# A transformer block with shared and routed experts on one core: expert weights loaded whole, the stage ahead of the tiles put in another order, and the weight and destination of each routed row formed on VectorE instead of GpSimd

## What is computed

```python
h = _layernorm(x) * (1 + ca) + sa
x = x + ga * attention(h)
h = _layernorm(x) * (1 + cb) + sb
out = silu(h @ sg.T) * (h @ su.T) @ sd.T                  # shared expert
probs = softmax(h @ wr.T + rb); scores, idx = top_k(probs, 2); scores /= scores.sum()
for e in range(7):
    out = out + w[..., e] * (silu(h @ rg[e].T) * (h @ ru[e].T) @ rd[e].T)
x = x + gb * out
```

## Time and profile before

| | |
|---|---|
| median of 3 runs | 798.48 us (797.54 to 799.52) |
| the profiled execution's own time | 797.6 us |
| its span in the trace | 795.9 us |
| busy: PE, DVE, ACT, POOL | 686.8, 573.4, 545.9, 342.0 us |
| attention / middle / tiles and the end | to 490 / 490 to 595 / 595 to 796 us |

### The profile page before, as it was taken

The page is one execution under the profiler, slowest core; times in us unless marked ns, Lnnn a source line. Parts: engine busy times, 40 slices in busy tenths (PEclk is TensorE's granted clock), DMA queues, the critical chain, the costliest instruction groups (busy, mean ns, idle before and its releaser), DMA issues.

```text
span 795.9 us, 18082 instructions
## 1 busy us (share of the span) xinstructions
PE 686.8 (86%) x5304; PEld 395.3 (50%) x5304; DVE 573.4 (72%) x2042; ACT 545.9 (69%) x1013; POOL 342.0 (43%) x551
## 2 busy tenths in 40 slices
PE   2986899999999999999999986678869989999970
PEld 1553123333333333333333434567659889999960
DVE  5797889999999999999999834574773323333543
ACT  2785259889989888989888788544325556666640
POOL 1367613232322322232322123235657887666652
PEclk9999569999999999999999999699999999999995
DMA  9246021111111111111110079202233322223425
GB/s 260 83 156 219 1 74 47 39 30 29 47 47 48 47 28 30 41 46 47 48 37 14 1 136 178 68 23 81 63 92 78 82 76 81 66 68 104 131 87 158
DMA packets 64760, 59.46 MB, mean 75 GB/s; under 512 B 10798, under 2 KB 52398, under 8 KB 64668
## 3 DMA queue, kind: packets, MB, share of 16 engines
q1 hardware_dynamic: 58924, 46.85, 23.3%
q0 software_dynamic: 4480, 9.64, 3.4%
q10 hardware_dynamic: 1264, 1.84, 0.7%
HBM read 33.57 MB, written 24.33 MB: 73 GB/s over the span
## 4 chain that ended last, share of the span: by engine, by line
PE 59%; DVE 18%; ACT 9%; issue 7%; DMA 3%; POOL 1%; SPq 1%; ACTq 1%; DVEq 0%; POOLq 0%
PE ps L1658 13%; PE ps L1602 10%; PE ps L1843 9%; PE ps L1681 7%; PE ps L1854 6%; DVE junk L1238 5%; ACT probs L973 5%; PE ps L1864 3%; PE ps L1758 2%; PE ps L1636 2%; DVE junk L1210 2%; PE ps L1750 2%; DMA routed_results_scratch<-y_s,s_dest 1%; PE ps L1831 1%; DVE rot L1193 1%
## 5 line engine op out<-in xcount | busy, mean ns | idle before, releaser
L973 ACT ACTIVATE probs<-ps 128x1024 f32<-128x1024 f32 (+1 forms) x320 | 285.5, 941 | 34.5 <-PE ps L1681 32.1
L1210 DVE CUSTOM_DVE_ANT_0 junk<-ps,tri 128x512 f32<-128x512 f32 (+3 forms) x512 | 218.5, 487 | 13.9 <-PE ps L1602 11.6
L1602 PE MATMUL ps<-ka,qa 61*128 61x256 bf16 (+3 forms) x788 | 186.7, 325 | 10.0 <-DVE rowmax L1210 3.0
L775 POOL TENSOR_SCALAR_AFFINE_SELECT probs<-probs 128x512 f32<-128x512 f32 x128 | 79.7, 634 | 191.8 <-ACT probs L973 191.8
L1658 PE MATMUL ps<-probs,v 128*32 128x512 f32 (+3 forms) x1536 | 157.7, 498 | 1.3 <-POOL probs L775 1.1
L1681 PE MATMUL ps<-qa,ka 64*128 64x512 bf16 (+3 forms) x768 | 144.6, 331 | 7.7 <-ACT probs L973 5.6
L1602 PEld LDWEIGHTS ps<-ka,qa 61*128 61x128 bf16 x788 | 53.0, 95 | 159.8 <-DVE rowmax L1210 80.4
L844 POOL DMA_INDIRECT routed_results_scratch<-y_s,s_dest x76 | 76.2, 1003 | 41.0 <-issue 35.0
L782 POOL DMA_INDIRECT slot_rows_scratch<-rows,slot x64 | 64.1, 1001 | 56.6 <-DVE slot L1393 30.1
L1243 DVE TENSOR_REDUCE leftmax<-ps 128x1 f32<-128x512 f32 x120 | 78.4, 686 | 8.5 <-PE ps L1602 8.5
L1532 DVE TENSOR_TENSOR hid_s<-sg,ps 128x352 f32<-128x352 f32 x76 | 39.6, 521 | 46.2 <-ACT sg L1087 46.0
(11 more groups left out here) (195 smaller groups left out, 1168.4 us busy)
## 6 DMA issues: line engine op xcount, KB each, us to landing
slot_rows_scratch<-cst SPq DMA_DIRECT2D x1, 5396.0 KB, 36.1
srow<-slot_rows_scratch SPq DMA_DIRECT2D x76, 71.0 KB
k_parts_scratch<-qk_parts SPq DMA_DIRECT2D x12, 320.0 KB, 2.7
ka<-k_parts_scratch SPq DMA_DIRECT2D x32, 120.0 KB
q_parts_scratch<-qk_parts SPq DMA_DIRECT2D x12, 256.0 KB, 2.6
qa<-q_parts_scratch SPq DMA_DIRECT2D x32, 96.0 KB
ka<-k_parts_scratch SPq DMA_DIRECT2D x32, 80.0 KB
xs<-in_x SPq DMA_DIRECT2D x4, 512.0 KB, 9.4
```

Of the source, the lines that this page charges most:

```text
L775: nc.gpsimd.affine_select(out=p, in_=p, compare_op=ALU.is_ge, fill=0.0, base=0, pattern=[[0, HQ], [1, T]], channel_multiplier=-1).then_inc ...
L973: nc.scalar.activation(probs[(n * NS + s) % 4][:, 2 * h:2 * h + 2, 0:UNTIL[s] - FROM[s]], ps[:, 2 * h:2 * h + 2, FROM[s]:UNTIL[s]], ACT.Ex ...
L1210: last = V.tensor_tensor_reduce(out=junk[:, bank - 5, at:at + w], in0=ps[:, bank, at:at + w], in1=tri[:, CH - w:CH], scale=1.0, scalar=LOW ...
L1602: last = MM(ps[:, bank, at:at + w], qa[m][g0:g0 + KS, c0 + q * T:c0 + (q + 1) * T], ka[m][g0:g0 + KS, d0 + k0:d0 + k0 + w], start=True, st ...
```

## The change

- Middle: the lists of calls of TensorE, VectorE and ScalarE are written in another order. `gate_up` and `silu` may now be called for single pieces, and `hidden(0, 0)` comes before the routing of the first half.
- Weights: `w_whole` holds all seven experts (it lies where `w_lo` lies, which is formed in place). SyncE loads all of it in one go, behind the end of attention and ahead of `wd`; nothing is loaded late in attention, and no load waits for a buffer.
- Tiles: the register load, `s_weight` and `s_dest` go from GpSimd to the end of VectorE's step, one step list of VectorE beginning at -2. Destinations are now computed as floating point and written as integers, and the constants are stored so.

```diff
+        w_whole = sb("w_whole", [D, NE, 2, NI], at=before_y)
+        before_y.close()
         w_lo = sb("w_lo", [D, NE, 2, NI], F32R, at=moe)
...
-            load_expert(0)
-            load_expert(1)
-
             sp.wait_ge(s_ring_free, len(BY_DVE))
+            for e in range(NE):
+                sp.dma_start(w_whole[:, e, 0, :], sw_g_d[1 + e, :, :]).then_inc(s_wraw[e], 16)
+                sp.dma_start(w_whole[:, e, 1, :], sw_u_d[1 + e, :, :]).then_inc(s_wraw[e], 16)
             for c, (i0, w) in enumerate(IC):
                 sp.dma_start(wd[0:w, :, c, :], sw_d_d[1:EX, i0:i0 + w, :].rearrange("e p h -> p e h")).then_inc(s_wd, 16)
-            for e in range(2, NE):
-                load_expert(e)
...
-            pool.wait_ge(s_expert, GRP)
-
             def slot_step(i, r):
-                at = tile(i, r, -2)
-                if at:
-
-                    t, j, times = at
-                    pool.wait_ge(s_srow[j], 16 * times + 16)
-                    e = pool.value_load(expert[0:1, bass.ds(t, 1)], min_val=0, max_val=NE - 1)
-                    nc.gpsimd.tensor_copy(s_weight[:, bass.ds(t, 1)], srow[:, j, bass.ds(D + e, 1)])
-                    d = (r + 2) % SU
-                    needs(pool, s_y_out[j], 16 * (times - SU // SB + 1))
-                    nc.gpsimd.tensor_tensor(s_dest[:, d:d + 1], srow[:, j, bass.ds(D + NE + e, 1)].bitcast(I32),
-                                            cst[:, bass.ds(CST["spare"][0] + t, 1)].bitcast(I32), ALU.add).then_inc(s_meta, 1)
...
+                at = tile(i, r, -2)
+                if at:
+                    t, j, times = at
+                    dve.wait_ge(s_srow[j], 16 * times + 16)
+                    e = dve.value_load(expert[0:1, bass.ds(t, 1)], min_val=0, max_val=NE - 1)
+                    V.tensor_copy(s_weight[:, bass.ds(t, 1)], srow[:, j, bass.ds(D + e, 1)])
+                    d = (r + 2) % SU
+                    needs(dve, s_y_out[j], 16 * (times - SU // SB + 1))
+                    V.tensor_tensor(s_dest[:, d:d + 1], srow[:, j, bass.ds(D + NE + e, 1)],
+                                    cst[:, bass.ds(CST["spare"][0] + t, 1)], ALU.add).then_inc(s_meta, 1)
                 if isinstance(i, int) and first_combine <= r < first_combine + 3 * GC:
                     combine(*divmod(r - first_combine, 3))
-            slot_steps(dve, -1, ST + 1, slot_step)
+            dve.wait_ge(s_expert, GRP)
+            slot_steps(dve, -2, ST + 1, slot_step)
...
             pe.wait_ge(s_ws_lo, 1)
             pe.wait_ge(s_wds_gated, len(IC))
-            gate_up(0, (0, 1))
+            gate_up(0, (0,))
+            router(2)
             router(3)
+            pe.wait_ge(s_x2, 2)
+            gate_up(0, (1, 2))
             turn_normalised(4)
-            gate_up(0, (2,))
+            gate_up(1, (0, 1))
+            down(0)
+            turn_normalised(5)
             counts(0)
```

More of the change, by code:

```diff
@@ L293, in adaln_block @@
         ws_lo = sb("ws_lo", [D, 2, NI], F32R, at=att)
-        w_raw = sb("w_raw", [D, 2, 2, NI], at=att)
+        w_raw = sb("w_raw", [D, 2, NI], at=att)
         wds = sb("wds", [128, len(IC), D], at=att)
@@ L426, in adaln_block @@
         s_exp7 = sem("s_exp7")
-        s_wraw = [sem(f"s_wraw{m}") for m in range(2)]
+        s_wraw = [sem(f"s_wraw{e}") for e in range(NE)]
         s_whi = sem("s_whi")
@@ L1017, in first_part @@
             def first_part(e):
-                act.wait_ge(s_wraw[e % 2], 32 * (e // 2 + 1))
-                nc.scalar.activation(w_hi[:, e, :, :], w_raw[:, e % 2, :, :], ACT.Copy).then_inc(s_whi, 1)
+                act.wait_ge(s_wraw[e], 32)
+                nc.scalar.activation(w_hi[:, e, :, :], w_whole[:, e, :, :], ACT.Copy).then_inc(s_whi, 1)
             def exp7(g):
@@ L1023, in exp7, with silu @@
                 nc.scalar.activation(prob[:, GTILES[g], :], logit[:, GTILES[g], :], ACT.Exp).then_inc(s_exp7, 1)
-            def silu(n):
-                for c, (i0, w) in enumerate(IC):
+            def silu(n, pieces=range(len(IC))):
+                for c in pieces:
+                    i0, w = IC[c]
                     g = n * len(IC) + c
@@ L1276, in chunk, with attended @@
                 return slice(n * CG, (n + 1) * CG)
-            b = B - 1
-            for u in range(2):
-                n = 2 * b + u
+            def attended(u):
+                n = 2 * (B - 1) + u
                 dve.wait_ge(s_proj, u + 1)
```

187 lines of the change are left out of this document (99 added, 88 removed).

## The result

Measured were **790.2 us** (median of 7 runs, 787.3 to 795.0) against 799.1 us for the kernel before in the same comparison: ratio 0.989, 95% interval 0.988 to 0.991. The sign was right and 790.2 lies in the range, but the gain is 8.5 to 9 us where 16 were forecast. The profiled execution took 790.4 us (before 797.6), its span is 788.3 us (before 795.9), so 7.6 us have to be found in the traces, and 8.4 of the forecast gain are missing there.

A forecast was written before the change was run, and what follows sets the result against it. Bounds: waits round a TensorE, ScalarE, VectorE ring in the middle; TensorE's pace in the tiles, GpSimd between tiles 12 and 23. Middle -15.4, GpSimd -1.4, VectorE +0.8 give -16.0: 797.6 becomes 781.6, about 782 us with 0.9 added; range 771 to 793.

The forecast's parts named there:

- First `hid`, 506.5: Middle: the first `hid` starts at 506.5 instead of 514.73, with logits at 506.0 and 0.5 us of `softmax_shift`.
- VectorE's work behind it, 63.7: Middle: VectorE's work and small gaps from the first `hid` to the last `xs` come to 63.7 us.
- VectorE's waits, 9 us: Middle: VectorE waits 3 to 4 us for `down`, 4 for `silu`, 1 to 2 at hand-overs: 9 us.
- priced at 1.3: Middle, ScalarE: a fifth function table load ahead of the second `hid` costs 1.3 us, within the 9 us of waits.
- Stop of TensorE behind `down(7)`: End of the middle: TensorE stands long during VectorE's list behind `slots(1)`, at no cost because VectorE is at work.
- GpSimd, -1.4 us: Tiles: GpSimd's step falls from 2.77 to 2.57 us but starts later; 5.6 us lost instead of 7.0.
- VectorE in the tiles, +0.8 us: Tiles: VectorE's new work is hidden except 0.5 us in nine last steps adding `combine` and 0.3 at tile 0.
- Weights loaded whole, 0: Middle: loading all 14 weight transfers from about 490 costs nothing, as each lands before it is read.
- The ring keeps its waits: Middle: new lists move the stops instead of filling them; end at up to 590.7, time 788 to 794; chance 0.13.
- The first half's scatters: Rival: these scatters hold the tiles, landing at 573 to 575 against 579; at 1.4 us each, 786; chance 0.08.
- the bound of the tiles: Rival: VectorE's register load sequence exceeds 1.6 us and sets the tile pace; slower from 1.8 us; chance 0.05.
- The shared port: Tiles: VectorE's new operations hold up GpSimd's scatters by 0.2 us in 19 steps, 3.8 us more, 786; chance 0.04.

The follow-up runs named there:

- rows_later: The changed kernel with GpSimd waiting for chunk 3's `h_lo` before it scales the rows of chunks 2 and 3; 786.6 us, ratio 0.9848.
- six_third: The changed kernel with counts_later, logits4_early, rows_later, `combine` ahead of `hid_s`, five `w_lo` moved earlier and second-half row scatters thinned; 774.2 us, ratio 0.9692.
- counts_later: The changed kernel with TensorE's `counts(1)` behind `down(5)` instead of ahead of `gate_up(6, (1,))`; 786.6 us, ratio 0.9838.
- logits4_early: The changed kernel with VectorE's `logits(4)` and `hidden(2, 0)` ahead of `slots(0)`; 789.1 us, ratio 0.9877.
- exp_first: The changed kernel with `exp7(0)` ahead of `silu(0, (0,))` on ScalarE and `softmax_scale(0)` ahead of `hidden(0, 0)` on VectorE; 793.7 us, ratio 0.9935.
- tiles_alone: The kernel before with only the weight column and destinations moved from GpSimd to VectorE, middle and weights as before; 797.2 us, ratio 0.9975.
- tiles_undone: The changed kernel with the weight column and destinations formed on GpSimd again, new middle and whole weights kept; 792.5 us, ratio 0.9920.
- slots1_early: The changed kernel with VectorE's `slots(1)` directly behind `starts(1)` and `experts(1)` ahead of `hidden(7, 2)`; 788.5 us, ratio 0.9871.

## Where the prediction was right and where it was wrong

The sign was right and the gain half of what was forecast. The step that failed is VectorE's waits in the middle; the others are smaller.

- **First `hid`, 506.5: measured 507.44.** 0.3 us of it is `softmax_shift`, 0.79 us from the logits to `hid` and not 0.5. The logits, at 506.65 and not 506.0, stand behind a step left out: GpSimd's `modulate_rows` now lies beside VectorE's variance, whose operations took 2.8 us more in all (3.7 instead of 0.9 in rows_later), and TensorE stood 1.51 us at 505.56 for ScalarE, which had stood 2.55 us for the variance. In the kernel before only one of these operations was stretched, to 1.04 us. The earlier trace rows had shown the two engines holding each other up, and I used it only as a rival for the scatters. Without it, and with TensorE at full clock, the first `hid` comes at 505.08 (rows_later), earlier than forecast; with TensorE at half clock it comes at 507.74 all the same (six_third).
- **VectorE's work behind it, 63.7: measured 62.4.** Off by 2%, and half of that is the wait of 0.75 us for `w_hi` at 591.60, which the earlier trace rows leaves out and the step therefore counted as work. The way of counting held: length less waits is 62.2 to 62.6 us in every kernel with this order.
- **VectorE's waits, 9 us: measured 14.7. This step failed, with 5.7 of the 8.4 missing us.** The waits for a `down` came as counted (3.4 us where 3 to 4 were said), those at hand-overs too (1.6 where 1 to 2 were); the mis-sized term is the waits for a `silu`, eight with 9.7 us where six or seven with 4 us were forecast. Going through the lists call by call I had `counts(1)` among the rival's reasons, but not in the count: it costs 3.9 us (counts_later), by TensorE's stop and the half clock behind it. `turn_normalised(6)` for `logits(4)` costs 1.0 us of length (logits4_early, without the 1.5 us of the clock behind `counts(1)`). The table loads, "priced at 1.3", cost VectorE two waits of 2.7 us, but only 0.6 us would be saved without both; the early `silu` is worth more than the fifth load costs (exp_first). A load lasts 1.28 us in each of its rows, with the next operation 1.29 us behind its start, so here the row and not the 2.66 us of the Trainium skill (ScalarE: Activation LUTs, What ACT_TABLE_LOAD costs) holds.
- **Stop of TensorE behind `down(7)`, "which costs nothing": the stretch behind it took 0.8 us more.** The stop is 3.51 us long instead of 1.07. Before and after, from the first transposition to y_s of tile 0 (columns as in the first window):

```profile
594.98:603.28 8.30, 6.84 (x34) 6.17 (x35) 2.40 (x7) 2.82 (x9) 7.01 (x17) 0.79 0.37 88
```

```profile
584.83:593.97 9.14, 7.83 (x34) 6.95 (x35) 3.23 (x13) 2.83 (x10) 6.72 (x8) 0.63 0.32 82
```

The granted clock is 0.63 instead of 0.79, and two products of tile 0 take 0.95 us instead of 0.59. It goes with the new middle: 8.47 us in tiles_alone, 9.05 in tiles_undone. The clock was missing in the step. That the long stop brought it is not shown: slots1_early has a stop of 1.07 us there, behind a `down` that ran at half clock, and takes 9.49 us, and six_third has one of 1.90 us and takes 9.08.
- **GpSimd, -1.4 us: measured -0.4.** Mechanism right, size off. The 2.57 us for a step measured 2.53; the 5.6 us of loss measured 6.9, since the first result was scattered 1.4 us later after the first y_s than forecast (the 1.2 us behind the cast and the two first scatters held up by `w_lo`, less the later y_s). Without the move it would have been 12.7 (tiles_undone): with the new middle the move is worth 5.8 us there, and only GpSimd's later start hides it.
- **VectorE in the tiles, +0.8 us: measured +2.2.** Steady steps are unmoved, as forecast (copy and sum end 0.52 us behind `hid_s`; the load runs under it). "Nine steps of at most 0.4, I take 0.5" measured 1.4 over tiles 64 to 72: `h_lo` is 0.32 to 0.44 us late in each such step, near the bound, and 0.17 us of it is lost each time. "TensorE needs [the rows] for the same tile's turn anyhow" held: at tile 65 TensorE stood 1.20 us for the rows, turned them at 732.69, and VectorE, which stood 1.85 us for the same rows, formed `h_lo` at 733.62, 0.28 us behind `h_hi`. But the step gave these rows no price of their own: TensorE's wait for them is 0.38 us before, 0.63 in tiles_undone, 1.12 in tiles_alone and 1.20 after, and with it tiles 61 to 64 go from 7.61 us over 7.85 and 8.39 to 8.45, 0.8 us that the forecast had at 0. Most of it came with the move; why the rows land late then, no run shows.
- **Weights loaded whole, 0:** ScalarE waited for none of them, as forecast; no run has this part alone.
- **The rivals.** "The ring keeps its waits" (0.13) gave 788 to 794, and named both calls; it was the case that came, with an end of the middle (584.6) between its 590.7 and my 579.2. The first half's scatters ended at 571.4, ahead of the second half's casts. VectorE was not the bound of the tiles. The shared port did act, but in the variance and at `w_lo`; GpSimd's steps beside `s_weight` and `s_dest` stayed at 2.53.

## What to carry over

Count a list engine by engine as work plus waits: the work can be worked out to 2%, so the care belongs to the waits, and each call that needs another engine's late result (`counts`, a transposition into a buffer that must be free) is to be put into the sum at its place, with a bound for the half clock that may or may not follow a stop of TensorE. Before a gain is put down to an edit, look where in the trace it arises: 1.5 us of logits4_early and of rows_later arise at a call that neither touched. When an engine is the bound of a stretch, ask also which of its work can be done later: with the row scatters thinned as one of six edits, tiles 0 to 23 lost 1.9 us instead of 6.9. When order changes, look at what two engines that share a way to memory now do side by side.
